# Small heads of a decoder in quarter steps, with masks as TensorE products and q and k split in their bank

## What is computed

```python
x = x + _L1_attn_ref(_layernorm(x), w_q, w_k, w_v, w_o)          # 16 heads of 16, causal
x = x + _L1_xattn_ref(_layernorm(x), ctx, wq, bq, wkv, bkv, wp, bp)  # 16 heads of 16, keys from the context, int8 roundings
x = x + _L2_attn_ref(_layernorm(x), Wq, Wk, Wv, Wo)              # 32 heads of 8 that share 8 heads of k and v, causal
```

## Time and profile before

| | |
|---|---|
| median of 3 runs | 2813.8 us |
| the profiled execution | 2822.94 us, span 2820.9 us |
| TensorE busy, share of the span | 2207.2 us, 78% |
| VectorE, ScalarE, GpSimd busy | 61%, 37%, 29% |
| mean granted clock of TensorE | 0.835 of full speed |
| L1Attn, from the span's start | 468 to 662 us, first exponential at 507 |
| L1Cross | 662 to 910 us, first exponential at 733 |
| L2Attn | 1001 to 1291 us, first exponential at 1036 |

### The profile page before, as it was taken

The page is one execution under the profiler, slowest core; times in us unless marked ns, Lnnn a source line. Parts: engine busy times, 40 slices in busy tenths (PEclk is TensorE's granted clock), DMA queues, the critical chain, the costliest instruction groups (busy, mean ns, idle before and its releaser), DMA issues.

```text
span 2820.9 us, 37045 instructions
## 1 busy us (share of the span) xinstructions
PE 2207.2 (78%) x12500; PEld 1564.5 (55%) x12509; DVE 1722.4 (61%) x4967; ACT 1036.5 (37%) x2368; POOL 814.9 (29%) x1357
## 2 busy tenths in 40 slices
PE   6889946886777468785459899689999999898792
PEld 4777824553453245543126576367777776675571
DVE  4655477544554956654867888656666666664532
ACT  2233313321221323222455756244544454443230
POOL 2122222221011213331000000145555555553344
PEclk9999968766786567756569999899999999999896
DMA  6000000000000030000000000200000000005453
GB/s 224 20 17 15 1 15 1 1 1 1 1 1 24 1 159 2 1 1 32 0 0 1 1 1 1 84 1 1 5 1 4 1 1 1 8 5 198 75 140 96
DMA packets 35051, 80.54 MB, mean 29 GB/s; under 512 B 4880, under 2 KB 21776, under 8 KB 32240
## 3 DMA queue, kind: packets, MB, share of 16 engines
q1 hardware_dynamic: 30016, 65.46, 6.3%
q0 software_dynamic: 4560, 12.46, 2.1%
q10 hardware_dynamic: 288, 0.26, 0.0%
HBM read 65.71 MB, written 10.35 MB: 27 GB/s over the span
## 4 chain that ended last, share of the span: by engine, by line
PE 23%; DVE 16%; ACT 6%; POOL 5%; issue 4%; DMA 1%; POOLq 0%; DVEq 0%; SPq 0%; ACTq 0%
PE ps L2085 4%; PE ps L2104 3%; DVE K L2519 3%; PE ps L2851 2%; DVE K L2508 2%; PE ps L2462 2%; POOL C L2735 2%; DVE K L2498 1%; ACT K L2654 1%; PE ps L2431 1%; PE ps L2455 1%; DVE X L1916 1%; ACT K L2655 1%; POOL K L3122 1%; PE ps L2872 1%
## 5 line engine op out<-in xcount | busy, mean ns | idle before, releaser
L1124 ACT ACTIVATE K<-ps 128x768 f32<-128x768 f32 (+1 forms) x128 | 110.4, 863 | 289.9 <-PE ps L967 289.6
L2133 DVE TENSOR_TENSOR_SCAN W<-W,ps 128x512 f32<-128x512 f32 x128 | 155.9, 1218 | 42.1 <-issue 24.5
L1076 DVE CUSTOM_DVE_ANT_0 K<-ps,K 128x128 bf16<-128x128 f32 (+1 forms) x384 | 114.4, 354 | 100.8 <-PE ps L952 100.2
L2085 PEld LDWEIGHTS ps<-K 128*128 128x128 f32 x1024 | 136.9, 196 | 65.8 <-issue 51.9
L2654 ACT ACTIVATE K<-ps,K 128x256 f32<-128x256 f32 x128 | 60.8, 475 | 304.0 <-DVE K L2498 304.0
L2462 PE MATMUL ps<-W,K 128*128 128x256 f32 x512 | 132.6, 405 | 41.9 <-DVE K L2519 35.3
L2730 POOL TENSOR_TENSOR K<-K 128x512 f32<-128x512 f32 x128 | 133.3, 1041 | 108.7 <-DVE K L2501 107.1
L2455 PE MATMUL ps<-W,K 128*128 128x512 f32 x256 | 125.4, 612 | 28.6 <-DVE K L2519 28.6
L2085 PE MATMUL ps<-K 128*128 128x128 f32 x1024 | 139.2, 280 | 8.1 <-DVE W L2133 8.1
L952 PE MATMUL ps<-K 32*128 32x256 bf16 (+1 forms) x1280 | 105.9, 307 | 49.0 <-DVE K L1076 35.7
L2462 PEld LDWEIGHTS ps<-W,K 128*128 128x128 f32 x512 | 100.3, 201 | 67.1 <-DVE K L2519 46.6
(11 more groups left out here) (521 smaller groups left out, 5775.2 us busy)
## 6 DMA issues: line engine op xcount, KB each, us to landing
W<-in_m SPq DMA_DIRECT2D x32, 256.0 KB, 4.6
results<-K SPq DMA_DIRECT2D x63, 128.0 KB
W<-in_wproj SPq DMA_DIRECT2D x1, 4096.0 KB, 12.6
W<-in_m SPq DMA_DIRECT2D x32, 128.0 KB, 5.1
W<-in_Wq SPq DMA_DIRECT2D x1, 2048.0 KB, 12.5
W<-in_Wo SPq DMA_DIRECT2D x1, 2048.0 KB, 16.8
W<-in_w SPq DMA_DIRECT2D x2, 1024.0 KB, 18.3
W<-K SPq DMA_DIRECT2D x4, 512.0 KB, 2.9
```

Of the source, the lines that this page charges most:

```text
L1076: m = e.tensor_tensor_reduce(self.junk[p][:, j, c0:c1], self.ps[j][:, c0:c1], self.maskq[:, m0:256], -1.0, -PAD, ALU.add, ALU.min, to[:, j ...
L1124: e.activation(to, made, ACT.Exp).then_inc(*self.up("exp"))
L2085: m = e.matmul(ps[1 + 2 * (n % 2)][:, b * 128:(b + 1) * 128], self.dtuT[h][:, i, b * 128:(b + 1) * 128], self.diag[s % 4][:, b * 128:(b + ...
L2133: e.tensor_tensor_scan(self.st[i % 3], self.a[i % 3], ps[1 + 2 * (i % 2)][:, :], 0.0, ALU.mult, ALU.add).then_inc(*sig.up("m scan"))
```

## The change

A step is now four quarters: scores in even ones, the transposed product in odd ones. Units are placed by the quarter, one at a time, and use banks 5 and 6 in turn; max, turn, flip, project and norm work shares bank 7 and one counter. The float32 rings and the splits are gone: the projection stays in its bank, a copy to bf16 is taken out, TensorE adds the negative of that part (a bf16 product of 512 columns with a negated, masked identity), the next copy is taken, and so on, one level a quarter: two such products for a q unit, two for an L1 k unit, three for an L2 k unit. Copies are by ScalarE, VectorE, ScalarE in turn. Both causal masks are bf16 products that open the accumulation of a bank: identity times mask for the scores, mask times identity for the transposed product, 256 columns for each of two heads. The maxima become plain reductions over two heads, two a half-step in the causal stages. The GpSimd selection and the wait for it go. The scale of q moves into the exponential.

```diff
-        self.f, self.U = a.ring(3, 512), a.ring(3, 512)
+        self.hi = a.ring(4, 512, dt=BF16)
+        self.minus = {name: a.new(128, dt=BF16) for name in self.MINUS}
...
+        at += [(8 * n - 1, "max", n, 0) for n in range(self.N // 2)]
...
+        units = sorted((4 * self.per * b + q, kind, b, c) for b in range(B) for kind, c, q in self.UNITS)
+        self.units, self.index = {}, {}
+        for u, (q, kind, b, c) in enumerate(units):
+            self.index[kind, b, c] = u
+            for n in range(len(self.LEVELS[kind])):
+                self.units.setdefault(q + n, []).append((u, kind, b, c, n))
...
     def pe(self, t):
-        for s in range(self.first_step, self.last_step):
-            for p in range(2):
-                if 0 <= s + self.LEAD < self.N:
-                    self.pe_scores(t, s + self.LEAD, p)
-                if 0 <= s < self.N:
-                    self.pe_probabilities(t, s, p)
-                if p == 0:
-                    for kind, b, c, u in self.at("unit", s):
-                        t.wait_ge(self.s("unit kept"), u)
-                        self.unit(t, kind, b, c).then_inc(*self.up("unit"))
-            if 0 <= s - 1 < self.N:
+        for q in self.quarters:
+            s, p, second = q // 4, q % 4 // 2, q % 2
+            if not second and 0 <= s + self.LEAD < self.N:
+                self.pe_scores(t, s + self.LEAD, p)
+            if second and 0 <= s < self.N:
+                self.pe_probabilities(t, s, p)
+            for u, kind, b, c, n in self.units.get(q, ()):
+                if n == 0:
+                    if u >= 2:
+                        self.wait_part(t, u - 2, self.last[u - 2])
+                    m = self.unit(t, kind, b, c, self.ps[5 + u % 2])
+                else:
+                    self.wait_part(t, u, n - 1)
+                    t.wait_ge(self.s("minus"), 1)
+                    m = t.e.matmul(self.ps[5 + u % 2][:, :], self.minus[self.LEVELS[kind][n - 1][2]], self.part(u, kind, b, c, n - 1),
+                                   start=False, stop=True, skip_group_check=True)
+                m.then_inc(*self.up("unit"))
...
+        if self.CAUSAL:
+            for j in range(2):
+                t.e.matmul(self.ps[j][:, :].rearrange("p (i n) -> p i n", n=256)[:, :, 0:128], self.g.identb,
+                           self.g.maskb.rearrange("p (i n) -> p i n", i=1).to_broadcast([128, 2, 128]), start=True, stop=False,
+                           skip_group_check=True)
...
+        if self.CAUSAL:
+            for j in range(2):
+                t.e.matmul(self.ps[2 + j][:, 0:256].rearrange("p (i n) -> p i n", n=128), self.g.maskb,
+                           self.g.identb.rearrange("p (i n) -> p i n", i=1).to_broadcast([128, 2, 128]), start=True, stop=False,
+                           skip_group_check=True)
...
-        t.wait_ge(self.s("chosen"), s + 1 if self.CAUSAL else 0)
...
+    def copy_parts(self, eng, q, who):
+
+        for u, kind, b, c, n in self.units.get(q, ()):
+            to, by, _ = self.LEVELS[kind][n]
+            if by == who:
+                eng.wait_ge(self.s("unit"), self.made[u, n])
+                if kind == "v":
+                    eng.wait_ge(self.s("quads"), self.per * (b - 1))
+                elif to not in ("hi", "mid"):
+                    eng.wait_ge(self.s("logits"), 2 * self.per * (b - self.SETS + 1))
+                self.copy_part(eng, u, kind, b, c, n, self.ps[5 + u % 2]).then_inc(*self.up("parts of " + who))
...
+        banks = self.g.PS[:, 0:1024]
         if self.CAUSAL:
-            v.wait_ge(v.own, v.n)
-            v.wait_ge(self.s("maximum"), 2 * s + p - 1)
-            for j in range(2):
-                for i, (c0, c1, m0) in enumerate(((0, 128, 128), (128, 384, 0))):
-                    m = e.tensor_tensor_reduce(self.junk[p][:, j, c0:c1], self.ps[j][:, c0:c1], self.maskq[:, m0:256], -1.0, -PAD,
-                                               ALU.add, ALU.min, to[:, j, i:i + 1])
+            for i, (c0, c1) in enumerate(((0, 128), (128, 384))):
+                m = e.tensor_reduce(to[:, :, i:i + 1], banks.rearrange("p (j k) -> p j k", j=2)[:, :, c0:c1], AX.X, ALU.max, negate=True)
         else:
-            m = e.tensor_reduce(to, self.g.PS[:, 0:1024].rearrange("p (j i k) -> p j i k", j=2, i=2), AX.X, ALU.max, negate=True)
+            m = e.tensor_reduce(to, banks.rearrange("p (j i k) -> p j i k", j=2, i=2), AX.X, ALU.max, negate=True)
...
-            if self.CAUSAL and 0 <= s < self.N:
-                p.wait_ge(self.s("exp"), 2 * s + 2)
-                T = self.T[s % 2][:, 0:2, :].rearrange("p k (h n) -> p (k h) n", n=128)
-                e.affine_select(T, T, [[0, 8], [1, 128]], ALU.is_ge, 0.0, base=0,
-                                channel_multiplier=-1).then_inc(*self.up("chosen"))
...
-        v.step(e.scalar_tensor_tensor(U, parts[0], mask, f, ALU.mult, ALU.add).then_inc(v.own, 1))
-        v.wait_ge(v.own, v.n)
-        if kind == "q":
-            v.step(e.tensor_copy(parts[0], U).then_inc(v.own, 1))
-            v.wait_ge(v.own, v.n)
-            e.scalar_tensor_tensor(parts[1], parts[0], mask, U, ALU.mult, ALU.add).then_inc(*self.up("split"))
-        else:
-            v.step(e.tensor_copy(parts[1], U).then_inc(v.own, 1))
-            v.wait_ge(v.own, v.n)
-            e.tensor_tensor(parts[2], U, parts[1], ALU.subtract).then_inc(*self.up("split"))
...
 class L1Attn(SmallHeads):
 
 
-    PER, VHEADS, DV, CAUSAL, QUANT, NEXT, WO, QMASK, PREPARED, SETS, MROWS = 16, 16, 16, True, False, 4, "wo1", 0, 0, 3, 1
-    UNITS = [("q", 0), ("k", 0), ("q", 2), ("k", 2), ("v", 0), ("v", 1)]
-    UNIT_STEPS = [-7, -7, -6, -6, -3, -2]
+    PER, VHEADS, DV, CAUSAL, QUANT, NEXT, WO, PREPARED, SETS, MROWS = 16, 16, 16, True, False, 4, "wo1", 0, 3, 1
+    UNITS = [("q", 0, -20), ("k", 0, -18), ("q", 2, -16), ("k", 2, -14), ("v", 0, -11), ("v", 1, -9)]
+    MINUS = {"low": 0, "high": 1, "all": -1.0}
+    LEVELS = {"q": [("hi", "act", "low"), (0, "dve", "low"), (1, "act", None)],
+              "k": [(0, "act", "high"), (1, "dve", "all"), (2, "act", None)], "v": [("v", "act", None)]}
+    SCALE = 0.25
...
-    UNITS = [("k", 0), ("q", 0), ("q", 2), ("q", 4), ("q", 6), ("v", 0), ("v", 1)]
-    UNIT_STEPS = [-8, -8, -7, -6, -5, -3, -2]
+    PER, VHEADS, DV, CAUSAL, QUANT, NEXT, WO, PREPARED, SETS, MROWS = 32, 8, 8, True, False, 7, "wo2", 0, 2, 2
+    UNITS = [("k", 0, -24), ("q", 0, -22), ("q", 2, -18), ("q", 4, -16), ("q", 6, -14), ("v", 0, -11), ("v", 1, -9)]
+    MINUS = {"half": 0, "odd": 2, "first": 3}
+    LEVELS = {"q": [("hi", "act", "odd"), (0, "dve", "odd"), (1, "act", None)],
+              "k": [("hi", "act", "half"), (0, "dve", "first"), ("mid", "act", "first"), ("last", "act", None)],
+              "v": [("v", "act", None)]}
```

461 lines of the change are left out of this document (200 added, 261 removed).

## The result

The changed kernel takes 2689.4 us, the median of four runs (2680.3 to 2695.4), against 2812.6 us for the kernel before in the same session: ratio 0.955, 95% interval 0.950 to 0.960, 4.5% faster. The profiled execution has a span of 2678.5 us, 142 less than before; it is the quickest of the four, so it shows somewhat more gain than the medians (123 us).

A forecast was written before the change was run, and what follows sets the result against it. TensorE at a low clock was taken to bound the three stages: 483.3 us of full-clock work, 580 busy at the expected clock, plus 123 idle gave 703, 29 less than 732. Forecast 2785 us, range 2730 to 2845.

The forecast's parts named there:

- sum of W: TensorE's busy time in the three stages, weighed at full clock: to rise by 74.7 us to 483.3.
- new idle time where TensorE waits for a level in the first batch of a stage: Uncovered copies between subtractions at the start of the three stages: 27 at 0.69 us, 19 us.
- its 53 us: Extra TensorE time for 492 new products if their weight loads were not hidden; an estimate from the skill's page, left out.
- the term of 123 us: TensorE's idle time in the three stages: 169.5 us less 47, bounds 100 and 150.
- named waits: TensorE's waits before score products and before projections in the three stages: 81.1 us, of which 66 were to go.
- The clock: Mean granted clock in L1Attn, L1Cross and L2Attn: to rise to 0.83, 0.83 and 0.79 as projections cover more of each.
- 703 of the forecast: Time of the three stages together: 580 us busy plus 123 idle, 29 less than 732.
- rival 1: Masks keep the three stages' clock full almost throughout: 2735 us at f = 0.8, 2711 at 0.9; chance 0.20.
- f: Share of time at full clock, 2c - 1 for mean clock c: expected 0.65 in the L1 stages, 0.58 in L2Attn.
- L2Attn no faster: Sign expected in the profile after: L2Attn at 292 us, against 290 before.
- GpSimd's selection: valued at 0 to 1 us: Dropping the 48 mask selections in the causal stages: worth 0 to 1 us, as they held TensorE for 0.6 us.
- Masks as 49.9 us in the path: 384 mask products on TensorE at 0.13 us: 16.6 us more in L1Attn, 33.3 in L2Attn.

The follow-up runs named there:

- before_three_parts: Kernel before with one q or k unit a step, masks as TensorE products with no GpSimd selection, and plain maxima: 2738.7 us, ratio 0.973.
- before_no_splits: Kernel before with VectorE's splits of q and k left out, lower parts constant and q scaled smaller: 2726.1 us, ratio 0.967.
- after_split_load: Changed kernel with three unread split-like VectorE operations behind each of VectorE's copies of a part: 2731.2 us, ratio 0.969.
- after_no_masks: Changed kernel without its 384 mask products, the causal stages computed without a mask: 2659.7 us, ratio 0.943.
- before_masks_by_tensor: Kernel before with both masks as TensorE products, plain maxima and no GpSimd selection, all else in the old order: 2790.9 us, ratio 0.989.
- after_one_bank: Changed kernel with one bank for the units in place of two, L2Attn's k unit a quarter earlier: 2759.1 us, ratio 0.979.

## Why the prediction was wrong, step by step

**Right.** TensorE and its clock bound the three stages. The price of each product held: a subtraction 0.23 us and a mask 0.13, both as forecast. The sum of W was forecast at 483 us and came out at 473. Waits before scores were to be under 15 us: 12.5. The new idle time where TensorE waits for a level in the first batch of a stage was to be 19 us: 21.7 were recorded there before the subtractions, and 0.6 in the loops. L1Cross, without masks, gained most (56 us). Plain maxima take 1.02 us a half-step, within 0.92 to 1.19. The Trainium skill's rule that a weight load hides only where row groups differ ("TensorE: Matmul & The Clock Gate", Part 3) was rated as not borne out, and the mask's 0.13 us agrees with leaving its 53 us out.

**The idle time: the term of 123 us was 45 too large.** The prediction removed 66 of the 81 us of named waits, added the levels and kept the other 88 us of idle time as they were. Of the 78 us that remain, 12.5 are waits before scores and some 24 waits for levels, so the rest shrank from 88 to about 42. It held the same cause in smaller pieces: the turn of the output rows waits on VectorE for 13.4 us in L2Attn of the kernel before (11.5 in before_three_parts, 6.1 in before_no_splits), so half of this wait goes with the splits alone. A cause that is removed takes all its waits with it, not only the two that were counted. What made up the rest of the 46 us was not taken apart.

**The clock: the step that failed most.** It was forecast at 0.83, 0.83 and 0.79, by counting how long the projections would cover each stage, and came out at 0.93, 0.87 and 0.92. Of the 109 us between the 703 of the forecast and the 594 measured, 45 are idle time, 12 the smaller W, and 52 the clock. L2Attn's 0.92 is past the 0.88 at which the prediction said that it would be wrong. The picture behind it, that projections lift the clock and it decays afterwards, was read from a stream full of gaps. The runs show another one: the gaps bring it down (746 us in after_split_load), and a TensorE with few gaps keeps it at full through a loop without masks (502 to 604 in after_no_masks), the last 35 us of it also without a q or k unit. The kernel before had it too. Ahead of the 51 us at half clock of the earlier trace rows stands this wait, and the clock fell at 580.9 us:

```profile
579.48 1.13 PE L1017 MATMUL ps<-W,K 128*128 128x256 f32 x4 [3.28 <-DVE X L1059]
```

**The argument against rival 1 was the misreading.** It said that dense small-head work alone did not raise the clock in the earlier trace rows, which is true, and took it for proof that such work can't hold it. The stretch at 581 us began at half clock, behind the wait above, and had no q or k projection, in or behind which the clock rose twice in the same loop (516 and 553.6 us). Rising and being kept are two questions, and that row answers only the first. Rival 1, the clock nearly full throughout, was the outcome: its times were 2735 for f = 0.8 and 2711 for 0.9; the measured f are 0.86, 0.74 and 0.84, and with the idle time of 78 us in place of 123 the first of these is 2690. Its reason was half right. Masks keep the clock up in the old order, but in the new one L1Attn doesn't need them.

The Trainium skill has the case in "TensorE: Matmul & The Clock Gate", Part 1, under the second failure mode: frequent short idle times between groups of products make the clock swing, though each product at full clock runs as fast as ever. The trace agrees: the score products take 0.67 us before and after, in the earlier trace rows and at 521.29 us, and what differs is how much of them ran at 1.14. The same part's rule that activity releases the throttle does not cover, 47.5 us busy in 51 at half clock.

**L2Attn no faster: it became 48 us faster.** Forecast at 292 us, it took 241.5. This was the sum of W +43 against idle and clock terms, both too small: its idle time went from 64 to 28, not 47, its clock to 0.92, not 0.79. **L1Attn** was forecast at 195 and took 162.6, and a single line of spacing brings it there.

**GpSimd's selection: valued at 0 to 1 us.** That was right for the old order and wrong for the new: 23 us of difference to the masks on TensorE, 52 to none. The cover that the prediction named, the next step's products, is half gone in the new order. "The mask moves from an idle engine to the bound one" is true and still the cheaper place.

**Masks as 49.9 us in the path.** As work 50; as time of the stages 29.5.

**What stays open.** How the 49 us between before_three_parts and the changed kernel divide between the subtraction in the bank, the quarters and the second bank was not tried piece by piece; with one bank the new order takes 2759 us, more than the 2739 of before_three_parts, so the quarters and the subtraction pay only with two. Why L2Attn's clock needs the masks more than L1Attn's wasn't tried either.

## What to carry to other kernels

Where TensorE is the bound and its clock averages well below full, look first for gaps of one to three microseconds and for what makes the engine behind them late: without the splits the stages of the kernel before lost 102 us, for 38 us less of idle time. Ask for each gap where it stands, since waits of 0.7 us took the clock in the start of a stage and not in its loop. Move work to the bound engine if that removes a wait, but price the same work again in the new order, since covers change with it. And when a row shows that something does not raise the clock, ask whether it would keep it.

## What the runs showed of the chip

- The clock depended on what went before. A stream of row-tiled bf16 products of 32 rows, with the products by v and without a q or k unit, stayed at 0.50 where it was entered at half clock (busy 47.5 of 51 us) and at 1.00 where it was entered at full (32.5 of 35 us, 569 to 604 in after_no_masks). At half clock the same products take longer, so the two busy shares don't compare the streams.
- With two full-height bf16 products ahead of each group (before_masks_by_tensor) the clock stayed at 1.00 from 519 to 618 us with TensorE busy for 87.1 of 99 us, where the kernel before was at 0.50 from 536.5 to 553.6 and from 580.9 us on. In its two causal stages no rise of the clock came behind such products alone; each came in or behind fp32 projections.
- At 746 us in after_split_load one wait of 2.23 us went with the fall from 1.00 to 0.50, and products slowed from 0.83 to 1.46 us for 17 us. In the kernel before a wait of 3.28 us went with the fall at 580.9 us.
- Waits of 0.7 to 0.9 us before projections (after_one_bank) went with a clock of 0.58 in the start of L1Attn and left it at 1.00 in its loop.
